# Attention with local windows and compressed entries, and a product in fp8: narrower turns of P, entries alternating with feed-forward products, batch 0's products moved into batch 3

## The chip, the cores and the metric

The kernel runs on one core of one Trainium2 chip. The metric is its time on the device in microseconds (us): the median over runs.

## The reference

For each of 4 batches of 1024 rows and 512 columns, x is normalised by row to xn, and the output is x + attention(xn) + product(xn).

```python
q  = rope(rmsnorm(xn @ Wq + bq))                 # 16 heads of 128
e  = softmax-weighted sums of 4 rows of xn       # 256 "entries"
ck, cv = rope(rmsnorm(e @ Wk + bk)), e @ Wv + bv
sparse = softmax of the 8 largest causal q.ck, times cv
lk, lv = rope(rmsnorm(xn @ Wlk + blk)), xn @ Wlv + blv
local  = softmax over own and previous block of 128 keys, times lv
attention = (sparse + local) / 2 @ Wo + bo
product   = fp8(xn * s) / s @ (fp8(input2 * s1) / s1)
```

## The kernel before, in words

The work is cut into 256 *units*, numbered u: batch u // 64, pair of heads (u // 8) % 8, block of 128 rows u % 8. A software pipeline runs over steps s. In step s TensorE projects q and lk of unit s (`proj_qk`, 24 matmuls of 512 columns in two halves: L520 to L522, four of each to a unit), turns and projects for unit s - 1 (`tr`, `proj_v`), and does the scores of s - 2, the turn of the probabilities P of s - 3 (`turn_p`, L576), the values of s - 4 (L591 with cv, the compressed values, and L594 with v) and the output product of s - 5 (`out_proj`, L606 to L608). f32 factors are kept as two rounded halves, hi and lo, multiplied in three matmuls; P, the entries and the values are plain f32, where one matmul is issued as two records with a load (LDWEIGHTS) each; turns are one.

Beside the units there are *tiles*: 32 blocks of 128 rows of x, eight to a batch. Batch 0's are prepared in steps -9 to 2. Tile t of a later batch is prepared one batch ahead, every seventh step from `tile_base(t)` on, by the delays in `LAGS` and, for four tiles together, `BLOCK_LAGS`: statistics (`norm_stats`, DVE), the power -0.5 of the variance (`power_x`, POOL), normalising, turning x, entries (`et`: four f32 matmuls with xt as the stationary and 32 columns of wm as the moving operand, L636), then ck and cv of a block (`ckv`, `turn_ck`). The feed-forward product of a tile is four bf16 matmuls of 512 columns (`ffn`, L662) on a quantised tile; `ffn_base(t)` sets its step, with `excess` and `rejoin` (DVE) and `quant_nan` (POOL) ahead of it and `init` (DVE) behind, which adds it to x. For tiles 0 to 7 it is done in batch 0 (steps 13, 20, ... 62) and added into `acc`, the sum of the batch in SBUF; for later tiles into `ini`, which is parked in HBM and loaded into `acc` at the batch's start. Input 2 is quantised in steps 4 to 9 in the same way.

During batch 0 the weights are split into halves (POOL `split` for Wq, Wlk, Wlv; ACT `hi_wo` and DVE `lo_wo` for Wo, in step 8g + 4 of group g) through the two buffers `wr`, and copied to HBM (`keep`, `keep_wo`), from where batches 1 to 3 fetch them.

Each engine executes its own list in order, written out as a loop over s; semaphores join them. Positions matter here. DVE's step: masks and maxima of s - 2 (`mask_max`, `max8`, `neg_max`), `lo_x` and `init`, `lo_c` of s - 4, `put_qk` (adds the bias to the projection), `lo_qk`, the sums for the norms, `add_out` of s - 5, and last the tile's statistics, `normalise`, `lo_wo`, `excess`, `rejoin`. POOL's: `rope_b`, `rope_rest`, `quant_nan`, `power_x`, `power_qk` (which ScalarE's `kscale` needs), `keep_8` and `normalise_p` of s - 2, which fills P's unused columns with zeros first, then `split`. ACT's: `put_et`, `hi_c`, the exponentials, copies, `kscale`, `hi_wo`, `cast_w2`. PSUM has a bank T for turns (`tr`, `turn_x`) and a bank Y for the output product, entries, ckv and feed-forward; `free` holds what TensorE has to wait for before it writes a bank. SP issues all of the large DMAs, in the order of its own loop.

Of the kernel before, what the change touches and what calls it, by code (L numbers as in the profile page):

```python
# [70 lines left out]

def unit_at(s, lag):
    return s - lag if 0 <= s - lag < NU else None


def tile_base(t):
# [5 lines left out]
        "max": (2, 2, 3), "ew": (3, 3, 4), "wm": (3, 3, 4), "et": (3, 4, 6), "park": (3, 3, 4)}  # L82
# [4 lines left out]
def tile_at(s, stage):  # L87
    for t in range(NTT):
        if tile_base(t) + LAGS[stage][min(t // 4, 2)] == s:
            return t  # L90
    return None


def block_at(s, stage):
    for k in range(NTT // 4):
        if tile_base(4 * k + 3) + BLOCK_LAGS[stage][min(k, 2)] == s:
            return k
    return None


def ffn_base(t):

    return 10 + 7 * t if t < 8 else tile_base(t) + 5
# [46 lines left out]
def build(nc, x, Wq, bq, Wcmp, bcmp, Wk, bk, Wv, bv, Wlk, blk, Wlv, blv, qnw, knw, Wo, bo,  # L150
# [9 lines left out]
    with ctx:  # L160
# [58 lines left out]
        kepto = nc.dram_tensor("kepto", (NG, 2, 2, 128, 512), F32, kind="Internal").ap()  # L219
        inis = nc.dram_tensor("inis", (NTT, 128, 512), F32, kind="Internal").ap()  # L220
# [98 lines left out]
        def run_sync(e):  # L319
# [100 lines left out]
            def store(u):  # L420
                b, i = u // 64, u % 8
                if b == 0:
                    e.wait_ge(S["bo0"], i + 1)
                else:
                    e.wait_ge(S["acc"], u + 1)
                e.dma_start(out[b, i * 128:(i + 1) * 128, :], acc[:, i, :]).then_inc(S["d_o%d" % i], 16)
# [32 lines left out]
            for s in range(FIRST, LAST):  # L459
# [34 lines left out]
            for i in range(NT):  # L494
                e.wait_ge(S["d_o%d" % i], 16 * NB)

        def run_tensor(e):
# [70 lines left out]
            def turn_p(u, h):  # L570
                a = 2 * u + h
                e.wait_ge(S["norm"], a + 1)
                if a >= 2:
                    e.wait_ge(S["p"], a - 1)
                for n, k in enumerate(pblocks(u)):
                    last = e.transpose(bP[h][:, n * 128:(n + 1) * 128], P[:, u % 2, h, k * 128:(k + 1) * 128], ident)  # L576
                last.then_inc(S["pt"], 1)

            def values(u, h):
                b, i = u // 64, u % 8  # L580
                ts_ = units_of(u)
                if h == 0:
# [48 lines left out]
            def entries(t):  # L631
                e.wait_ge(S["wm"], t + 1)
                if free["Y"]:
                    e.wait_ge(S[free["Y"][0]], free["Y"][1])
                for kt in range(KT):
                    last = e.matmul(bY[:, kt * 32:(kt + 1) * 32], xt[:, t % XR, kt * 128:(kt + 1) * 128], wm[:, :],  # L636
                                    start=True, stop=True)
                last.then_inc(S["et"], 1)
                free["Y"] = ("put_et", t + 1)
# [36 lines left out]
            for s in range(LAST):  # L676
# [12 lines left out]
                if tile_at(s, "et") is not None:  # L689
                    entries(tile_at(s, "et"))  # L690
                if ffn_at(s, 3) is not None:
# [21 lines left out]
        def run_scalar(e):  # L713
# [115 lines left out]
            def put_et(t):  # L829
# [3 lines left out]
                e.activation(et[:, :, (t % 4) * 32:(t % 4 + 1) * 32], bY[:, 0:128].rearrange("p (k c) -> p k c", k=KT),  # L833
# [45 lines left out]
            for s in range(LAST):  # L879
# [38 lines left out]
                if 4 <= s < 4 + KT:  # L918
                    cast_w2(s - 4)
# [3 lines left out]
        def run_vector(e):  # L923
# [105 lines left out]
            def add_out(u):  # L1029
# [8 lines left out]
                if u < 64 and u + 5 >= ffn_base(u % 8) + 3:  # L1038
                    e.wait_ge(S["init"], ffn_pos(u % 8) + 1)
# [77 lines left out]
            def init(t, s):  # L1117
                a = rows(t)
                e.wait_ge(S["ff"], ffn_pos(t) + 1)
                e.wait_ge(S["xn"], t + 1)  # L1120
                if t < 8:
                    done = [u for u in range(t, 64, 8) if u < s - 5]
                    if done:
                        e.wait_ge(S["acc"], done[-1] + 1)
# [55 lines left out]
            for s in range(LAST):  # L1180
# [3 lines left out]
                if u2 is not None:  # L1184
# [5 lines left out]
                    neg_max(u2)  # L1190
                if tile_at(s, "lo") is not None:
                    lo_x(tile_at(s, "lo"))
                if ffn_at(s, 3) is not None:
                    init(ffn_at(s, 3), s)
# [41 lines left out]
                if 5 <= s < 5 + KT:  # L1236
                    excess(s - 5)
                    rejoin(s - 5)
# [6 lines left out]
        def run_gpsimd(e):  # L1245
# [31 lines left out]
            def normalise_p(u, h):  # L1277
                C, top_ = width(u), 128 * (u % 8 // 4 + 1)
# [88 lines left out]
            for s in range(FIRST, LAST):  # L1367
# [10 lines left out]
                if 6 <= s < 6 + KT:  # L1378
                    quant_nan(s - 6)
# [97 lines left out]
```

## Time and profile before

| | |
|---|---|
| median of 3 runs | 2566.69 us (2566.32 to 2568.03) |
| the profiled execution | 2566.6 us, span 2564.8 us |
| granted TensorE clock, mean | 0.997 |
| PE busy | 2515.7 us (98%) |
| PEld, DVE | 2216.1 us, 1984.2 us (77%) |
| ACT, POOL | 1652.2 us (64%), 1565.7 us (61%) |
| DMA | 220.74 MB, 25.6% of 16 engines' time |

The span is the time from the first to the last instruction on the core. PE is TensorE's matmuls and PEld its weight loads, which overlap them; DVE is VectorE, ACT ScalarE, POOL GpSimd, SP SyncE. L576 is line 576 of the kernel. Batch 0 begins at 39.55 us (unit 0), batch 1 at 686.6, batch 2 at 1310.1, batch 3 at 1933.6.

### The profile page before, as it was taken

How to read it: one execution, taken by the hardware profiler on the slowest of the kernel's cores; microseconds unless marked ns; L12 is line 12 of the kernel's file. 1: busy time of each engine (PE TensorE's matmuls, PEld its weight loads, DVE VectorE, ACT ScalarE, POOL GpSimd, SP SyncE). 2: the span in 40 equal slices, each digit the busy share in tenths (PEclk: the TensorE clock that was granted, in tenths of full speed). 3: DMA queues.
4: the chain of work that ended last, by engine and by line, in shares of the span. 5: the costliest groups of instructions: out<-in, count | busy, mean ns of one | idle time of the engine just before them, and what ended most of it. 6: DMA issues, size and time to landing. Idle time of an engine off the chain costs nothing. (4 is left out here: it accounts for less than half of the span.)

```text
span 2564.8 us, 54971 instructions
## 1 busy us (share of the span) xinstructions
PE 2515.7 (98%) x15288; PEld 2216.1 (86%) x15320; DVE 1984.2 (77%) x6309; ACT 1652.2 (64%) x4674; POOL 1565.7 (61%) x2766
## 2 busy tenths in 40 slices
PE   6999999999999999999999999999999999999998
PEld 5888888888888888888888888888888888888887
DVE  6888888888878778777877778777877776676775
ACT  4666666566666666666666666666666666666665
POOL 5777777776676555555556655555556655555554
PEclk9999999999999999999999999999999999999999
DMA  3532233224332212022243122122143221122101
GB/s 109 169 104 71 96 104 115 89 70 135 116 125 87 86 56 91 30 99 79 86 147 115 43 87 87 59 87 65 65 132 122 81 71 63 38 71 71 61 11 50
DMA packets 168291, 220.74 MB, mean 86 GB/s; under 512 B 17842, under 2 KB 89012, under 8 KB 167988
## 3 DMA queue, kind: packets, MB, share of 16 engines
q1 hardware_dynamic: 167412, 216.96, 25.6%
q8 instruction: 126, 2.06, 0.3%
q14 instruction: 177, 1.45, 0.2%
q10 hardware_dynamic: 576, 0.26, 0.0%
HBM read 156.35 MB, written 60.82 MB: 85 GB/s over the span
## 5 line engine op out<-in xcount | busy, mean ns | idle before, releaser
L1298 POOL TENSOR_TENSOR t<-raw,tB 128x128 f32<-128x128 f32 x512 | 227.4, 465 | 592.2 <-DVE raw L930 591.8
L1252 POOL TENSOR_TENSOR r<-ss,mh 128x4 f32<-128x4 f32 x256 | 286.6, 1120 | 260.4 <-DVE ss L947 260.3
L779 ACT ACTIVATE ch<-bVC,blT 128x128 fp32r<-128x128 f32 x512 | 159.7, 363 | 435.8 <-PE bVC L594 435.0
L520 PE MATMUL bQK<-wh,xh 128*128 128x512 f32 x1024 | 426.7, 417 | 0.8 <-DVE raw L930 0.8
L521 PE MATMUL bQK<-wl,xh 128*128 128x512 f32 x1024 | 404.1, 395 | 0.0
L522 PE MATMUL bQK<-wh,xl 128*128 128x512 f32 x1024 | 401.9, 393 | 0.0
L975 DVE CUSTOM_DVE_ANT_0 P<-bS,cst 128x256 f32<-128x256 f32 (+1 forms) x512 | 203.7, 398 | 157.3 <-PE bS L568 156.8
L536 PE MATMUL bVC<-wh,xh 128*128 128x256 f32 x1024 | 311.1, 304 | 5.7 <-DVE cl L1024 5.7
L746 ACT ACTIVATE P<-P,nm,r 128x256 f32<-128x256 f32 (+1 forms) x512 | 295.3, 583 | 0.0
L740 ACT ACTIVATE raw<-raw,r 128x128 f32<-128x128 f32 x512 | 177.9, 395 | 177.0 <-POOL r L1252 172.4
L538 PE MATMUL bVC<-wh,xl 128*128 128x256 f32 x1024 | 289.8, 283 | 0.0
L537 PE MATMUL bVC<-wl,xh 128*128 128x256 f32 x1024 | 289.7, 283 | 0.0
L1024 DVE SCALAR_TENSOR_TENSOR cl<-bVC,blT,ch 128x128 fp32r<-128x128 f32 x512 | 155.7, 346 | 169.3 <-ACT ch L779 168.7
L1287 POOL TENSOR_SCALAR P<-P,rs 128x256 f32<-128x256 f32 (+1 forms) x512 | 257.7, 503 | 20.1 <-POOL P L1274 10.9
L957 DVE TENSOR_TENSOR qkl<-bT,qkh 128x512 fp32r<-128x512 f32 x256 | 177.1, 692 | 115.8 <-ACT qkh L718 115.3
L594 PEld LDWEIGHTS bVC<-pt,v 128*128 128x128 f32 x1920 | 254.5, 191 | 13.4
L594 PE MATMUL bVC<-pt,v 128*128 128x128 f32 x1920 | 255.5, 275 | 0.0
L726 ACT ACTIVATE pt<-bP 128x512 f32<-128x512 f32 (+2 forms) x512 | 239.9, 523 | 2.5 <-PE bP L576 2.4
L576 PEld LDWEIGHTS bP<-cst,P 128*128 128x128 f32 x1728 | 204.6, 141 | 35.9 <-POOL P L1288 0.9
L522 PEld LDWEIGHTS bQK<-wh,xl 128*128 128x128 f32 x1024 | 192.8, 188 | 44.7
L576 PE MATMUL bP<-cst,P 128*128 128x128 f32 x1728 | 231.2, 273 | 0.2 <-POOL P L1288 0.2
L606 PE MATMUL bY<-woh,ch 128*128 128x512 f32 x512 | 224.1, 438 | 6.3 <-DVE ini L1125 4.8
(144 smaller groups left out, 6941.2 us busy)
## 6 DMA issues: line engine op xcount, KB each, us to landing
wh<-kept SPq DMA_DIRECT2D x144, 256.0 KB, 4.1
wl<-kept SPq DMA_DIRECT2D x144, 256.0 KB, 4.5
kept<-wh SPq DMA_DIRECT2D x48, 256.0 KB, 3.1
kept<-wl SPq DMA_DIRECT2D x48, 256.0 KB, 3.3
woh<-kepto SPq DMA_DIRECT2D x48, 256.0 KB, 3.3
wol<-kepto SPq DMA_DIRECT2D x48, 256.0 KB, 3.8
out<-acc SPq DMA_DIRECT2D x32, 256.0 KB, 2.2
ini<-in_hidden_states SPq DMA_DIRECT2D x24, 256.0 KB, 4.6
```

Source lines behind the costliest of these rows:

```text
L520: e.matmul(bQK[:, :], a, b, start=kt == 0, stop=False)
L521: e.matmul(bQK[:, :], a, bl, start=False, stop=False)
L522: last = e.matmul(bQK[:, :], al, b, start=False, stop=kt == 3)
L536: e.matmul(bVC[:, 0:256], a, b, start=kt == 0, stop=False)
L537: e.matmul(bVC[:, 0:256], a, bl, start=False, stop=False)
L538: last = e.matmul(bVC[:, 0:256], al, b, start=False, stop=kt == KT - 1)
L576: last = e.transpose(bP[h][:, n * 128:(n + 1) * 128], P[:, u % 2, h, k * 128:(k + 1) * 128], ident)
L594: last = e.matmul(dst, v_[:, t % 4, h, :], pt[:, h, n * 128:(n + 1) * 128], start=False, stop=n == len(ts_) - 1 and h == 1)
L726: e.activation(pt[:, h, 0:n], bP[h][:, 0:n], ACT.Copy).then_inc(S["p"], 1)
L746: e.activation(pl, pl, ACT.Exp, scale=r4[:, u % 4, 2 * h:2 * h + 1], bias=nm[:, u % 4, h, 1:2], accum_out=su[:, u % 4, h, 1:2]).then_inc(S ...
L1252: e.tensor_tensor(r4[:, u % 4], ss[:, u % 4], mh[:, 0:4], ALU.pow).then_inc(S["r4"], 1)
L1287: e.tensor_scalar(pl, pl, rs[:, u % 4, h, 1:2], 0.5, ALU.mult, ALU.mult)
```

## The change

- `turn_p` turns only `last_rows(u)` columns of P's last block (68, 68, 96, 128 for u % 4 = 0 to 3; 128 in units 0, 1 and 4), `values` multiplies with as many rows of cv and pt, and `normalise_p` fills only up to there.
- Entries of tiles from 8 on go to bank T and two steps later (lag 8 for 6), but for the last tile of a batch. Where they meet a feed-forward product in one step, `entries_ffn` issues both in turn, an f32 entry matmul and then a 512-column bf16 one. Even blocks from the second batch on are two steps later.
- The feed-forward products of tiles 0 to 7 are at steps 201, 208, ... 250. Batch 0's sum goes to `part` in HBM and comes back into `ini` for `init`; SP stores the result.
- `lo_wo` is in the next step behind `neg_max`; `keep_wo` is a step later. `power_x` is behind `normalise_p` in steps from 0 on.
- Input 2 is loaded and quantised two steps earlier.

```diff
+def last_rows(u):
+    return 128 if u in (0, 1, 4) else max(68, width(u) - 128 * (u % 8 // 4))

-        "max": (2, 2, 3), "ew": (3, 3, 4), "wm": (3, 3, 4), "et": (3, 4, 6), "park": (3, 3, 4)}
+        "max": (2, 2, 3), "ew": (3, 3, 4), "wm": (3, 3, 4), "et": (3, 4, 8), "park": (3, 3, 4)}
 def tile_at(s, stage):
+        early = 2 if stage == "et" and t >= 8 and t % 8 == 7 else 0
+        if tile_base(t) + LAGS[stage][min(t // 4, 2)] - early == s:
 def block_at(s, stage):
+        late = 2 if k >= 2 and k % 2 == 0 else 0
+        if tile_base(4 * k + 3) + BLOCK_LAGS[stage][min(k, 2)] + late == s:
 def ffn_base(t):
-    return 10 + 7 * t if t < 8 else tile_base(t) + 5
+    return 64 * (NB - 1) + 6 + 7 * t if t < 8 else tile_base(t) + 5

 # SP
+                    e.dma_start(part[i], acc[:, i, :]).then_inc(S["d_o%d" % i], 16)   # batch 0
+            def fetch_part(t):
+                e.wait_ge(S["d_o%d" % t], 16)
+                if t < 2:
+                    e.wait_ge(S["d_is"], 16 * (NTT - 8))
+                else:
+                    e.wait_ge(S["d_f"], 16 * (t - 1))
+                e.dma_start(ini[:, t % 2, :], part[t]).then_inc(S["d_i%d" % (t % 2)], 16)
+            def store_whole(t):
+                e.wait_ge(S["init"], ffn_pos(t) + 1)
+                e.dma_start(out[0, t * 128:(t + 1) * 128, :], ini[:, t % 2, :]).then_inc(S["d_f"], 16)
-                    if kind == "o" and split_at + 1 == s:
+                    if kind == "o" and split_at + 2 == s:
                         keep_wo(gi, c)
-                if 2 <= s < 2 + KT:
-                    load_w2(s - 2)
+                if 0 <= s < KT:
+                    load_w2(s)
+                if t is not None and t < 8:            # t = ffn_at(s, 5)
+                    store_whole(t)
+                if ffn_at(s, 1) is not None and ffn_at(s, 1) < 8:
+                    fetch_part(ffn_at(s, 1))

 # TensorE
+                    r = last_rows(u) if k == pblocks(u)[-1] else 128
+                    last = e.transpose(bP[h][0:r, n * 128:(n + 1) * 128], P[:, u % 2, h, k * 128:k * 128 + r], ident)
+                        r = last_rows(u) if n == i // 4 else 128
+                        e.matmul(bVC[:, 256:512], cv[0:r, b % 2, n, :], pt[0:r, :, c], start=n == 0, stop=False)
+            def entries_ffn(t, f):
+                e.wait_ge(S["wm"], t + 1)
+                e.wait_ge(S[free["T"][0]], free["T"][1])
+                e.wait_ge(S["q8"], 4 + ffn_pos(f) + 1)
+                e.wait_ge(S[free["Y"][0]], free["Y"][1])
+                for kt in range(KT):
+                    c = slice(kt * 128, (kt + 1) * 128)
+                    m = e.matmul(entries_of(t)[:, kt * 32:(kt + 1) * 32], xt[:, t % XR, c], wm[:, :], start=True, stop=True)
+                    if kt == KT - 1:
+                        m.then_inc(S["et"], 1)
+                    last = e.matmul(bY[:, :], q8[:, ffn_pos(f) % QR, c], w2q[:, kt, :], start=kt == 0, stop=kt == KT - 1)
+                last.then_inc(S["ff"], 1)

 # ScalarE, VectorE, GpSimd
-                if 4 <= s < 4 + KT:
-                    cast_w2(s - 4)
+                if 2 <= s < 2 + KT:
+                    cast_w2(s - 2)
                     neg_max(u2)
+                for q, c in enumerate(CHUNKS):
+                    if c[0] == "o" and c[3] == s - 1:
+                        lo_wo(q)
                 if tile_at(s, "lo") is not None:
-                for q, c in enumerate(CHUNKS):         # at the end of the step
-                    if c[0] == "o" and c[3] == s:
-                        lo_wo(q)
-                C, top_ = width(u), 128 * (u % 8 // 4 + 1)
+                C, top_ = width(u), 128 * (u % 8 // 4) + last_rows(u)
-                if tile_at(s, "power") is not None:
+                if s < 0 and tile_at(s, "power") is not None:
                     power_x(tile_at(s, "power"))
                     normalise_p(u2, 1)
+                if s >= 0 and tile_at(s, "power") is not None:
+                    power_x(tile_at(s, "power"))
```

`excess`, `rejoin` and `quant_nan` of input 2 move by two steps with `cast_w2`; `init` takes `ini` for all tiles.

## Rows read from the trace of the kernel before

**Rows 1.** Busy us and instructions by stretch: PE, PEld, DVE, ACT, POOL; PEclk, DMA, GB/s.
```profile
39.55:686.60 647.05, 624.10 (x3738) 542.20 (x3753) 532.27 (x1614) 413.41 (x1168) 465.92 (x746) 0.99 0.31 104
1933.60:2545.00 611.40, 611.33 (x3746) 543.38 (x3746) 435.25 (x1461) 391.91 (x1111) 338.45 (x650) 1.00 0.19 64
```

**Rows 2.** The same view, of L520 on TensorE alone, in six stretches.
```profile
39.55:114.89 75.34, 14.04 (x32) 0.94 0.43 141
114.89:199.73 84.84, 13.78 (x32) 0.97 0.28 92
199.73:686.60 486.87, 79.77 (x192) 1.00 0.30 100
765.74:842.06 76.32, 13.29 (x32) 1.00 0.22 73
842.06:1310.09 468.03, 79.79 (x192) 1.00 0.25 82
2012.74:2087.44 74.70, 13.29 (x32) 1.00 0.18 61
```

**Rows 3.** Weight loads by line: busy us, mean ns of one | idle before.
```profile
L576 PEld LDWEIGHTS bP<-cst,P 128*128 128x128 f32 x1728 | 204.6, 141 | 35.9 <-POOL P L1288 0.9 <-issue 0.2
...
L591 PEld LDWEIGHTS bVC<-pt,cv 128*128 128x128 f32 x768 | 138.8, 189 | 21.0 <-ACT pt L726 3.6 <-issue 2.3
...
L662 PEld LDWEIGHTS bY<-w2q,q 128*128 128x128 bf16 x128 | 10.0, 98 | 12.7 <-issue 4.2
```

**Rows 4.** TensorE in time, a unit of batch 3: start, us, line, op.
```profile
2114.50 1.03 PE L576 MATMUL bP<-cst,P 128*128 128x128 f32 x8
...
2115.49 0.28 PE L537 MATMUL bVC<-wl,xh 128*128 128x256 f32 x1
2115.61 0.28 PE L538 MATMUL bVC<-wh,xl 128*128 128x256 f32 x1
```

**Rows 5.** TensorE in time, around the entries of a tile.
```profile
834.32 0.97 PE L636 MATMUL bY<-wm,xt 128*128 128x32 f32 x8
835.12 0.68 PE L591 MATMUL bVC<-pt,cv 128*128 128x256 f32 x2
835.64 0.61 PE L594 MATMUL bVC<-pt,v 128*128 128x128 f32 x4
```

**Rows 6.** TensorE in time, around a feed-forward product.
```profile
923.02 0.81 PE L662 MATMUL bY<-w2q,q 128*128 128x512 bf16 x3
923.67 1.03 PE L591 MATMUL bVC<-pt,cv 128*128 128x256 f32 x4
924.53 0.72 PE L594 MATMUL bVC<-pt,v 128*128 128x128 f32 x5
```

**Rows 7.** Waits of TensorE: total us, times, longest.
```profile
PE bY L606 <- DVE ini L1125: 4.8, 4, 3.1
```

**Rows 8.** Engines in time, units 44 and 45; idle before in brackets.
```profile
493.37 0.56 POOL L1256 TENSOR_TENSOR st<-st,mh 128x1 f32<-128x1 f32 x1 [2.71 <-DVE st L1055]
494.94 0.70 ACT L740 ACTIVATE raw<-raw,r 128x128 f32<-128x128 f32 x2 [4.14 <-POOL r L1252]
496.19 1.40 DVE L1045 TENSOR_TENSOR wol<-wr,woh 128x512 fp32r<-128x512 f32 x2 [2.90 <-ACT woh L789]
499.93 0.47 PE L606 MATMUL bY<-woh,ch 128*128 128x512 f32 x1 [3.08 <-DVE ini L1125]
```

**Rows 9.** Engines in time, units 60 and 61, then 9, then 8.
```profile
656.82 1.40 DVE L1045 TENSOR_TENSOR wol<-wr,woh 128x512 fp32r<-128x512 f32 x2 [1.26 <-ACT woh L789]
661.34 0.63 PE L546 MATMUL bT<-cst,raw 128*128 128x128 f32 x4 [2.20 <-DVE xsl L1074]
...
136.16 0.51 PE L536 MATMUL bVC<-wh,xh 128*128 128x256 f32 x1 [1.81 <-DVE cl L1024]
...
120.54 0.72 ACT L811 ACTIVATE a<-ini,isc 128x512 fp8e4<-128x512 f32 x1 [1.85 <-DVE qb L1098]
```

**Rows 10.** DMA issues: KB of one, median us to landing.
```profile
wr<-in_Wlv SPq DMA_DIRECT2D x16, 256.0 KB, 3.9
```

More of the change, by code:

```diff
@@ L219, in build @@
         kepto = nc.dram_tensor("kepto", (NG, 2, 2, 128, 512), F32, kind="Internal").ap()
+        part = nc.dram_tensor("part", (NT, 128, 512), F32, kind="Internal").ap()
         inis = nc.dram_tensor("inis", (NTT, 128, 512), F32, kind="Internal").ap()
@@ L282, in logits_of, with entries_of @@
             return (bY if t >= FIRST_TILES else bS[1])[:, 0:128]
+        def entries_of(t):
+            return (bY if t < 8 else bT)[:, 0:128]
         def bias_of(u, h):
@@ L423, in store @@
                     e.wait_ge(S["bo0"], i + 1)
-                else:
-                    e.wait_ge(S["acc"], u + 1)
-                e.dma_start(out[b, i * 128:(i + 1) * 128, :], acc[:, i, :]).then_inc(S["d_o%d" % i], 16)
+                    e.dma_start(part[i], acc[:, i, :]).then_inc(S["d_o%d" % i], 16)
+                    return
+                e.wait_ge(S["acc"], u + 1)
+                e.dma_start(out[b, i * 128:(i + 1) * 128, :], acc[:, i, :]).then_inc(S["d_o%d" % i], 16)
+            def fetch_part(t):
+                e.wait_ge(S["d_o%d" % t], 16)
+                if t < 2:
+                    e.wait_ge(S["d_is"], 16 * (NTT - 8))
+                else:
+                    e.wait_ge(S["d_f"], 16 * (t - 1))
[3 more added lines that the diff above has]
+                e.dma_start(out[0, t * 128:(t + 1) * 128, :], ini[:, t % 2, :]).then_inc(S["d_f"], 16)
             load_acc(0)
@@ L632, in entries @@
                 e.wait_ge(S["wm"], t + 1)
-                if free["Y"]:
-                    e.wait_ge(S[free["Y"][0]], free["Y"][1])
+                bank = "Y" if t < 8 else "T"
+                if free[bank]:
+                    e.wait_ge(S[free[bank][0]], free[bank][1])
                 for kt in range(KT):
-                    last = e.matmul(bY[:, kt * 32:(kt + 1) * 32], xt[:, t % XR, kt * 128:(kt + 1) * 128], wm[:, :],
+                    last = e.matmul(entries_of(t)[:, kt * 32:(kt + 1) * 32], xt[:, t % XR, kt * 128:(kt + 1) * 128], wm[:, :],
                                     start=True, stop=True)
                 last.then_inc(S["et"], 1)
-                free["Y"] = ("put_et", t + 1)
+                free[bank] = ("put_et", t + 1)
+            def entries_ffn(t, f):
[10 more added lines that the diff above has]
+                last.then_inc(S["ff"], 1)
+                free["T"] = ("put_et", t + 1)
+                free["Y"] = ("init", ffn_pos(f) + 1)
             def ckv(k):
@@ L688, in run_tensor @@
                     ckv(block_at(s, "kv"))
-                if tile_at(s, "et") is not None:
+                if tile_at(s, "et") is not None and ffn_at(s, 3) is not None:
+                    entries_ffn(tile_at(s, "et"), ffn_at(s, 3))
+                elif tile_at(s, "et") is not None:
                     entries(tile_at(s, "et"))
-                if ffn_at(s, 3) is not None:
+                elif ffn_at(s, 3) is not None:
                     ffn(ffn_at(s, 3))
@@ L1037, in add_out @@
                     e.wait_ge(S["bo"], u // 64 * 8 + u % 8 - 7)
-                if u < 64 and u + 5 >= ffn_base(u % 8) + 3:
-                    e.wait_ge(S["init"], ffn_pos(u % 8) + 1)
                 e.tensor_tensor(a, bY[:, :], a, ALU.add).then_inc(S["acc"], 1)
@@ L1115, in weights4, with init @@
                                 ALU.mult).then_inc(S["wm"], 1)
-            def init(t, s):
-                a = rows(t)
+            def init(t):
+                a = ini[:, t % 2, :]
                 e.wait_ge(S["ff"], ffn_pos(t) + 1)
-                e.wait_ge(S["xn"], t + 1)
                 if t < 8:
-                    done = [u for u in range(t, 64, 8) if u < s - 5]
-                    if done:
-                        e.wait_ge(S["acc"], done[-1] + 1)
+                    e.wait_ge(S["d_i%d" % (t % 2)], 16 * (t // 2 + NTT // 2 - 1))
+                else:
+                    e.wait_ge(S["xn"], t + 1)
                 e.scalar_tensor_tensor(out=a, in0=bY[:, :], scalar=isc[:, 4:5], in1=a, op0=ALU.mult,
@@ L1193, in run_vector @@
                 if ffn_at(s, 3) is not None:
-                    init(ffn_at(s, 3), s)
+                    init(ffn_at(s, 3))
                 if u4 is not None:
@@ L1235, in run_vector @@
                     rejoin(KT + ffn_pos(ffn_at(s, 1)))
-                if 5 <= s < 5 + KT:
-                    excess(s - 5)
-                    rejoin(s - 5)
+                if 3 <= s < 3 + KT:
+                    excess(s - 3)
+                    rejoin(s - 3)
                 if s == 0:
```

11 lines of the change are left out of this document (4 added, 7 removed), and 2 rows, old and new, of the table SIGNALS.

## The prediction

> **What bounds the kernel.** I read the engines' busy times by stretch first [rows 1]. TensorE is busy 611.33 of 611.40 us in batch 3 and 624.10 of 647.05 us in batch 0; VectorE, the next, has 435 and 532 us. So only TensorE's own work and its stalls cost time, and the stalls lie in batch 0. Second I count work periods by the projection's matmuls, four L520 to a unit [rows 2]: eight units take 74.70 us where nothing is added (batch 3), and units 16 to 63 of batch 0 take 486.87 us where units 80 to 127 of batch 1, with the same tiles in the same places, take 468.03. Third come loads and matmuls of single groups [rows 3 to 6], for what each edit is worth on a full TensorE, and last the waits and two places in batch 0 where a wait travels through the engines to TensorE [rows 7 to 9].
>
> **Narrower turns.** For 189 units (three quarters of 256, less three exempt ones) the last block of P is turned with 68 or 96 columns as the stationary operand instead of 128, in both heads: 378 turns, 19,096 columns fewer. The moving operand stays the identity's 128 columns. The eight turns of a unit start at 2114.50; L537 is at 2115.49, and a 256-column matmul ahead of it takes 0.12 (2115.49 to 2115.61), so the eight took 0.87, 0.109 each [rows 4]. Is that the load or the stream? The entries' matmuls move only 32 columns, so there the load sets the pace: eight of them from 834.32, and L591 with two matmuls of 0.215 ends at 835.64, so 835.21 - 834.32 = 0.89, 0.111 each (0.215 is 0.86/4, the four L591 of the next group) [rows 5, 6]. A turn's load is listed with 141 ns where an ordinary f32 load has 189 [rows 3]: 0.048 shorter. So a turn's load takes about 0.111 - 0.048 = 0.063 of the 0.109, and the rest of the pace is the stream of 128 identity columns, which stays. Bounds: if the 0.109 were all load and in proportion to the columns, 19,096 x 0.109/128 = 16.3 us would go; on the other side nothing excludes a loss, priced below. I take 0, since the load's own row is nearest. The values' matmul with fewer rows of cv keeps its 128 stationary and 256 moving columns: 0. The fill of P on GpSimd gets shorter; it is off the path, hidden by TensorE.
>
> The Trainium skill, "TensorE: Matmul & The Clock Gate", section "LDWEIGHTS", says the opposite of my choice: a load takes the stationary's column count over 1.2 GHz. By that sentence a 68-column load takes 57 ns instead of 107, and the turns would give some 16 us. Its 107 ns agrees with the entries' 0.111, but the listed turn load is shorter than that rule allows for 128 columns, and no row here has fewer.
>
> **Entries alternating with feed-forward products.** Tiles 8 to 31 now have their entries in the step of their feed-forward matmuls, but for the last tile of each batch (its entries stay two steps earlier): 7 x 3 = 21 pairs. Apart they cost 0.89 (above) and 4 x 0.216 = 0.87 (L662: 923.67 - 923.02 = 0.65 for three) [rows 6]: 1.76. Interleaved, the first entry load of each round is hidden behind the 512-column product before it. On the path are the second entry load, 0.111, the bf16 load and the product, 0.216. The bf16 load is listed with 98 ns against 189 [rows 3], 0.091 less, so about 0.02 of its own. A round is 0.35, four are 1.39 to 1.42. Gain 0.34 x 21 = 7.1. Bounds: with the bf16 load at its full 0.098, 4 x 0.425 = 1.70 and 1.3 us in all; with it free, 4 x 0.327 and 9.5 us. f32 and bf16 already follow each other in [rows 6] without a gap, so I see no loss. I take 7. New waits: bank T needs lo_qk of the step before, which is done before the scores; ScalarE's put_et now waits about 0.5 longer, ahead of hi_c, but hi_c waits for the values' matmuls behind the pair anyway.
>
> **Feed-forward of batch 0 moved to batch 3.** Eight products of 0.87, 6.9 us of TensorE, leave a batch and enter another: 0. Its VectorE work (excess, rejoin, init) and GpSimd work go where those engines have room: VectorE is busy 435 of 611 us there [rows 1]. Added DMAs: acc to part instead of out (the same), eight fetches and eight stores of 256 KB. On SP's queue fetch_part waits only for old transfers, and store_whole waits for an init two steps earlier; behind it stand weight fetches which have half a unit group of slack. 0.
>
> **Power and low halves in batch 0.** Units 16 to 63 are 486.87 - 468.03 = 18.84 us longer than their twins; seven products explain 7 x 0.87 = 6.1, so 12.7 is stall [rows 2]. The chain of its largest piece [rows 8]: GpSimd stands at power_x (L1256) for 2.71 us until VectorE's statistics at its step's end, so power_qk is late, ScalarE's kscale starts after 4.14 idle, hi_wo follows it, VectorE waits 2.90 for woh at the end of its step, begins the next step late, init is late, and TensorE's L606 stands 3.08. The change takes power_x behind keep_8 and normalise_p and the low halves into the next step behind neg_max, where VectorE otherwise idles ahead of lo_c. Both links are cut, and that init is gone too. The second piece, L546 2.20 behind xsl, has 1.26 of waiting for woh and 1.40 of lo_wo ahead of it in VectorE's order, and rejoin besides [rows 9]. What is late next: lo_wo's 1.4 now stands ahead of lo_x and lo_c in eight steps (I leave 0.5 there for some), and the weight buffer is released some 5 us later, so the next chunk lands at about +5 + 3.9 [rows 10] of a 10 us step, just when GpSimd wants to split it; chunk loads, keeps and load_ini queued behind it on SP shift with it. I take back 9 of 12.7, bounds 4 and 12.7. In batches 1 and 2 the same wait for ini costs L606 three times 1.7 in all beside the 3.1 [rows 7]; power_x's move takes 1.2 of it, bounds 0 and 1.7.
>
> **Input 2 quantised two steps earlier.** Units 8 to 15 take 84.84 against 76.32, of which one product 0.87: 7.7 us of stall, in part by a lower granted clock (0.97 of 2.4 GHz on average in the row), and units 0 to 7 take 75.34, more than eight full units, though the first four have no values and no output product [rows 2]. The rows show how: cast_w2 waits 1.85 for VectorE's qb, so hi_c, lo_c and L536 are late (1.81) [rows 9]. The same work now falls in units 2 to 7. There TensorE's units are shorter, so VectorE and ScalarE bind, but tile 8's statistics no longer meet it. It doesn't vanish; I take 6, bounds -2 and 12.
>
> **Sum.** 7 + 9 + 1.2 + 6 = 23.2 us off the profiled execution's 2566.6 (span 2564.8 and 1.8 around it), which lies 0.1 under the median of the runs: 2543.4. The forecast's own range adds the bounds in part: 2536 to 2551.
>
> **Rivals.** (1) Narrow loads shorten the turns, -16.3 more: 2527. For it: 0.109 and 0.111 are nearly one pace; against: the turn's load is listed 48 ns shorter. (2) Batch 0 gives little back: stalls of lo_wo ahead of lo_c, of the late chunk and of the quantisation in units 2 to 7 take the place of the old. Then 4 - 2 + 7 = 9 of gain: 2558. For it: VectorE is at 532 of 647 us in batch 0 [rows 1] and none of the work goes away but eight products'; against: both cut links are seen in [rows 8]. (3) Slower: a stationary operand narrower than 128 makes TensorE empty itself before and after it. Place: each narrow turn (two sides, two heads) and the cv matmuls (two sides), 6 times in 189 units, 1134 times. Price: a turn takes 0.27 from start to end and its pace is 0.109 (1.03 - 7 x 0.109) [rows 4], so 0.16 each: +181, 2725 us. It makes the change slower from 23/1134 = 0.02 us each. For it and against it there is no row: all stationary operands here have 128 columns.
>
> The Trainium skill, "TensorEngine Tiling (Array Packing)", section "Key Properties", says that changing the tiling mode drains TensorE; its modes are 128, 64 and 32, and 68 and 96 fit in 128 only, so by it (3) doesn't happen. No run here shows a drain.
>
> **Chances.** Forecast 0.57, (1) 0.22, (2) 0.16, (3) 0.05. The 8-in-10 range reaches into (1) and (2): 2522 to 2559. A measurement here tells 0.2%, 5 us; the first three cases all lie beyond it, but for a tail of (2): faster 0.93, same 0.02, slower 0.05.
>
> **What would show it.** Turns: eight in a unit still 0.87 long (0.77 by (1)), and eight plain units still 74.7 in late batch 3 (74.2 by (1)). Pairs: 1.4 in a step that had 0.87, none for entries alone in batches 1 and 2 but at the last tile. Batch 0: no 3 us hole at unit 45; units 16 to 63 about 486.9 - 6.1 - 9 - 7 x 0.34 = 469 (seven of the pairs lie in them). Units 0 to 15 153 instead of 160. Batch 3 6.9 longer. I am wrong if eight plain units change by over 0.1 us, if a pair takes 1.7, or if units 16 to 63 stay above 476.

## The result, and the profile after

The changed kernel takes 2547.93 us (2547.14 to 2548.24), the kernel before in the same session 2566.66 (2566.32 to 2568.03): ratio 0.9921 [0.991, 0.9933], 18.7 us faster. The forecast was 23.2 us, to 2543.4, so the time is 4.5 us above it and inside the likeliest case's own range.

The profiled execution took 2547.14 us, with a span of 2545.3 (before: 2564.8). First, as before, busy time against the span, from the page of the changed kernel.

```profile
PE 2509.3 (99%) x15320; PEld 2220.3 (87%) x15320; DVE 1975.3 (78%) x6309; ACT 1658.7 (65%) x4674; POOL 1540.3 (61%) x2702
```

TensorE's busy time fell by 6.4 (2515.7 before), the span by 19.5: two thirds of what went was standing. Where, the stretches tell. The next rows answer to [rows 2]: windows of the projection's first matmul, four to a unit (L520, now L550), with length, busy time, granted clock, DMA share and GB/s. They are units 0 to 7, 8 to 15, 16 to 63, 128 to 191, 200 to 207 and 208 to 215.

```profile
38.16:118.98 80.82, 15.10 (x32) 6.96 (x33) 0.87 0.36 123
118.98:195.19 76.21, 13.30 (x32) 6.07 (x33) 1.00 0.33 107
195.19:663.55 468.36, 79.90 (x192) 36.43 (x193) 1.00 0.31 104
1284.59:1905.13 620.54, 106.51 (x256) 48.55 (x257) 1.00 0.26 86
1984.29:2059.93 75.64, 13.33 (x32) 6.07 (x33) 1.00 0.20 67
2059.93:2136.42 76.49, 13.31 (x32) 6.07 (x33) 1.00 0.20 66
```

The same cuts in both traces add up to the whole difference (batches 1 and 2 were 623.5 each before; units 192 to 254 were 592.6, are 599.9; the tail is unit 255 and what follows):

| stretch | before | after | difference | forecast |
|---|---|---|---|---|
| until unit 0 | 39.55 | 38.16 | -1.4 | 0 |
| units 0 to 15 | 160.19 | 157.03 | -3.2 | -6.9 |
| units 16 to 63 | 486.87 | 468.36 | -18.5 | -17.5 |
| batches 1 and 2 | 1247.0 | 1241.6 | -5.4 | -6.0 |
| batch 3 to unit 254 | 592.6 | 599.9 | +7.3 | +6.9 |
| tail | 38.55 | 40.27 | +1.7 | 0 |

Two readings stand in it. Units 16 to 63 now take about what units 80 to 127 took in [rows 2] (468.03); those have got shorter too, to 465.93, so 2.4 of the 12.7 us of stall are left. Units 0 to 15 gave back half of what was forecast: units 8 to 15 fell from 84.84 to 76.21, units 0 to 7 rose from 75.34 to 80.82, at a mean clock of 0.87 for 0.94. Of this rise 2.9 lies in units 0 and 1 (19.01 before, 21.88 after). Unit 1 ran mostly at half clock in this profile (mean 0.58) and took 9.23 for 6.55; in kernels with the same code there it takes 6.6 to 9.7 (below), so this part is not the change's doing as far as these runs show. Units 2 to 15 by themselves fell from 141.17 to 135.15.

One shift of work is in the table, too: tile 8's entries (0.89) stood in unit 15 and now stand in unit 17, so units 0 to 15 lost them and units 16 to 63 got them.

The 3 us wait of L606 at unit 45 [rows 7, 8] is gone. Between unit 2 and unit 254 the longest waits of TensorE are now these, from the view of waits (L576 is the turn of ck and the q side of `tr`, L638 the first output matmul, L566 the projection of values). The first two are in unit 5, the third in unit 4; from unit 6 on none is over 0.4:

```profile
PE bT L576 <- DVE qkl L1201: 2.4, 1, 2.4
PE bY L638 <- DVE wol L1094: 2.1, 1, 2.1
...
PE bVC L566 <- DVE cl L1075: 0.6, 1, 0.6
```

The pair that `entries_ffn` makes, in time on TensorE (answers to [rows 5, 6]):

```profile
831.39 0.30 PE L682 MATMUL bT<-wm,xt 128*128 128x32 f32 x2
831.53 0.38 PE L685 MATMUL bY<-w2q,q 128*128 128x512 bf16 x1
831.75 0.30 PE L682 MATMUL bT<-wm,xt 128*128 128x32 f32 x2
...
832.60 0.38 PE L685 MATMUL bY<-w2q,q 128*128 128x512 bf16 x1
832.82 1.03 PE L623 MATMUL bVC<-pt,cv 128*128 128x256 f32 x4
```

From 831.39 to L623 at 832.82 it is 1.43 for what took 1.76 apart; a round is 0.36 (831.39 to 831.75). The turns (L576 is now L607) and the cv matmuls' loads, by form, with busy time and mean ns of one (answers to [rows 3]; L685 is the pair's bf16 load):

```profile
L607 PEld LDWEIGHTS bP<-cst,P 128*128 128x128 f32 x1350 | 168.2, 140 | 32.7 <-POOL P L1336 0.9 <-issue 0.2
...
L623 PEld LDWEIGHTS bVC<-pt,cv 68*128 68x128 f32 x250 | 46.5, 190 | 3.7
...
L607 PEld LDWEIGHTS bP<-cst,P 128*68 128x68 f32 x250 | 28.2, 113 | 2.8
...
L607 PEld LDWEIGHTS bP<-cst,P 128*96 128x96 f32 x128 | 16.3, 127 | 0.0
...
L685 PEld LDWEIGHTS bY<-w2q,q 128*128 128x128 bf16 x84 | 15.2, 181 | 0.0
```

The loads did get shorter: 140, 127 and 113 ns for 128, 96 and 68 columns, 0.45 ns a column. The next section asks whether anything follows from that.

### The profile page after: what moved, and what is told of

The parts are those of the page before. It is cut to its first block, busy times and chain, and to the rows that moved or that the text cites. A ratio compares the mean times of both kernels' runs of the same rounds, so it can differ in the third digit from the quotient of the medians.

```text
span 2545.3 us, 54963 instructions
## 1 busy us (share of the span) xinstructions
PE 2509.3 (99%) x15320; PEld 2220.3 (87%) x15320; DVE 1975.3 (78%) x6309; ACT 1658.7 (65%) x4674; POOL 1540.3 (61%) x2702
## 4 chain that ended last, share of the span: by engine, by line
PE 74%; DMA 0%; POOL 0%; issue 0%; SPq 0%; ACT 0%; DVE 0%; ACTq 0%; POOLq 0%; DVEq 0%
PE bQK L550 7%; PE bQK L551 7%; PE bQK L552 7%; PE bVC L626 6%; PE bP L607 6%; PE bVC L623 5%; PE bY L638 4%; PE bVC L566 4%; PE bVC L568 4%; PE bVC L567 4%; PE bY L639 4%; PE bY L640 4%; PE bT L576 3%; PE bS L598 3%; PE bS L597 3%; PE bS L596 3%
## 5 line engine op out<-in xcount | busy, mean ns | idle before, releaser
L550 PE MATMUL bQK<-wh,xh 128*128 128x512 f32 x1024 | 427.8, 418 | 0.8 <-DVE raw L981 0.8
L566 PE MATMUL bVC<-wh,xh 128*128 128x256 f32 x1024 | 310.6, 303 | 0.6 <-DVE cl L1075 0.6
L567 PE MATMUL bVC<-wl,xh 128*128 128x256 f32 x1024 | 289.5, 283 | 0.0
L1335 POOL TENSOR_SCALAR P<-P,rs 128x256 f32<-128x256 f32 (+1 forms) x512 | 246.7, 482 | 35.5 <-POOL P L1322 22.2
L607 PE MATMUL bP<-cst,P 128*128 128x128 f32 (+2 forms) x1728 | 231.1, 273 | 0.4 <-POOL P L1336 0.4
L607 PEld LDWEIGHTS bP<-cst,P 128*128 128x128 f32 (+2 forms) x1728 | 200.3, 135 | 35.5 <-POOL P L1336 0.9
L638 PE MATMUL bY<-woh,ch 128*128 128x512 f32 x512 | 224.9, 439 | 3.7 <-DVE wol L1094 2.1
```

The source lines that it names most:

```text
L550: e.matmul(bQK[:, :], a, b, start=kt == 0, stop=False)
L566: e.matmul(bVC[:, 0:256], a, b, start=kt == 0, stop=False)
L567: e.matmul(bVC[:, 0:256], a, bl, start=False, stop=False)
L607: last = e.transpose(bP[h][0:r, n * 128:(n + 1) * 128], P[:, u % 2, h, k * 128:k * 128 + r], ident)
L638: e.matmul(bY[:, :], a, woh[:, h, :], start=h == 0, stop=False)
L1335: e.tensor_scalar(pl, pl, rs[:, u % 4, h, 1:2], 0.5, ALU.mult, ALU.mult)
```

## The experiments

Each kernel is the changed one with one edit, unless said otherwise. The medians scatter (the kernel before had 2566.66 to 2569.89 beside the different runs), and with them the stretches at a lower clock near the two ends, so differences of a few us are read from stretches of units, each from one profiled execution. Where a unit's length is given without a row, it is the distance from its first projection matmul to the next unit's.

**Turns: full width.**

```diff
-    return 128 if u in (0, 1, 4) else max(68, width(u) - 128 * (u % 8 // 4))
+    return 128
```

> The changed kernel (2547.9 us) with P's last block turned and multiplied with all 128 columns and rows again, and filled with zeros to there. Theory: a turn's pace of 0.109 us is the stream of the identity's 128 columns, its load (listed 48 ns shorter than an ordinary f32 load) hides behind it. Then nothing changes: 2547.9 within 1 us, and eight turns of a unit take 0.87 us in both. Rival 1, the load sets the pace: 16 us slower, 2564. Third: the shorter zero fill on GpSimd is what counts, in batch 0 alone: 1 to 3 us slower, all of it in units 0 to 63.

2544.26 us, ratio 0.9907 [0.9893, 0.992]; its interval overlaps the changed kernel's. Windows of units 16 to 63 and 128 to 191:

```profile
194.47:662.39 467.92, 79.79 (x192) 36.42 (x193) 1.00 0.32 104
1282.67:1902.93 620.26, 106.38 (x256) 48.58 (x257) 1.00 0.26 86
```

They are 0.4 and 0.3 shorter than with narrow turns (468.36, 620.54), and units 200 to 207 take 75.59 for 75.64. So the narrow turns give nothing and cost about 0.05 in eight units, 1.5 us over 240 units; all of units 16 to 254 together differ by 1.8. The other 2.4 us of the span's difference (4.2) lie ahead of unit 16 and in the tail, where kernels with the same code there differ as much (below). Rival 1 falls, and the choice of 0 stands.

**Turns: a shorter stream.** If the moving operand paces a turn, shortening that one must show. On the kernel with full turns, from unit 8 on; it leaves out the last 60 queries of the block:

```diff
-    last = e.transpose(bP[h][0:r, n * 128:(n + 1) * 128], P[:, u % 2, h, k * 128:k * 128 + r], ident)
+    m = 68 if u >= 8 and k == pblocks(u)[-1] else 128
+    last = e.matmul(bP[h][0:r, n * 128:n * 128 + m], P[0:m, u % 2, h, k * 128:k * 128 + r], ident[0:m, 0:m],
+                    start=True, stop=True, is_transpose=True)
```

> The changed kernel with full turns (the run at 2544.3 us), and from unit 8 on the last block's turn moves 68 identity columns instead of 128, while its stationary keeps all 128 columns of P (68 of its 128 rows). It leaves out the last 60 queries of that block. 496 turns are touched. Theory: the stream of the moving columns is a turn's pace, so each takes (128 - 68) x 0.107/128 = 0.050 less until the load (0.063) binds, 0.045 to 0.050: 22 to 25 us faster, 2519 to 2522, and eight plain units of batch 3 go from 74.7 to 73.95. Rival 1, the load of 128 stationary columns sets the pace: no change, 2544.

2533.87 us, ratio 0.9869 [0.9854, 0.9884], 10.4 below full turns. Six turns of one unit, first in the kernel with full turns, then with the short ones, and the matmul behind them:

```profile
2121.69 0.82 PE L607 MATMUL bP<-cst,P 128*128 128x128 f32 x6
2122.26 0.36 PE L566 MATMUL bVC<-wh,xh 128*128 128x256 f32 x1
```

```profile
2112.64 0.72 PE L608 MATMUL bP<-cst,P 128*128 128x128 f32 x6
2113.17 0.36 PE L566 MATMUL bVC<-wh,xh 128*128 128x256 f32 x1
```

One turn of the two sides' last ones saves 0.044 (0.57 to 0.53), the other does not: from the second side's last turn to the second matmul behind it (L567) it is 0.23 in both. An ordinary load stands there, and I take its 0.111 [rows 5] for what paces. 248 units times 0.044 are 10.9. I had expected both to save. Units 128 to 191 are 2.75 shorter than with full turns, 0.043 a unit:

```profile
1277.33:1894.84 617.51, 106.37 (x256) 48.58 (x257) 1.00 0.26 86
```

What follows is that the 128 identity columns of the stream, not the load of P, hold a turn at 0.109; the load is hidden under them, and so was every column that the change took from it. The short turn's stationary also lost 60 of its 128 rows; its load is listed as before (140 ns for 141), and no run takes the two apart:

```profile
L608 PEld LDWEIGHTS bP<-cst,P 68*128 68x128 f32 x496 | 69.6, 140 | 2.8
```

**Turns: 64 columns.** Does a narrower stationary make TensorE empty itself (rival 3)?

```diff
-    return 128 if u in (0, 1, 4) else max(68, width(u) - 128 * (u % 8 // 4))
+    return 128 if u in (0, 1, 4) else max(64, width(u) - 128 * (u % 8 // 4))
```

> The changed kernel with 64 columns and rows in place of 68 where the last block has 32 or 64 entries. Theory: the load isn't the pace, and 64 is like 68: 2547.9 within 1 us. Rival 3, that a narrower stationary makes TensorE empty itself before and after: at 64, where 68 still counted as full width, it would show now, in 125 units, 6 times each, 0.16 us each: 120 us slower, 2668. A half of that, if only the turns or only the loads count, still is 2600 or more.

2594.15 us, ratio 1.0101 [1.0087, 1.0115]: 46 us slower than with 68. The loads by form, and loads in time around one unit's cv matmuls:

```profile
L607 PEld LDWEIGHTS bP<-cst,P 128*64 128x64 f32 x250 | 27.8, 111 | 2.8
...
L623 PEld LDWEIGHTS bVC<-pt,cv 64*128 64x128 f32 x250 | 36.8, 184 | 36.0 <-issue 36.0
```

```profile
2176.20 0.41 PEld L623 LDWEIGHTS bVC<-pt,cv 128*128 128x128 f32 x2
2176.94 0.29 PEld L623 LDWEIGHTS bVC<-pt,cv 64*128 64x128 f32 x2 [0.33 <-issue]
2177.57 0.97 PEld L626 LDWEIGHTS bVC<-pt,v 128*128 128x128 f32 x8 [0.33 <-issue]
```

The turns with 64 columns are not the cause: their loads idle 2.8 us in all, as those of 68 columns do. It is the values' matmul, whose stationary then has 64 rows. Its load stands 0.33 with nothing to wait for, and so does the first full load behind it; for 68 and 96 rows there is no such gap. Units 216, 217, 220 and 221, which have 64 rows, are 0.37 to 0.41 longer than with 68, the others not at all. So what rival 3 feared exists, on the rows, at 64, at some 0.2 for each of two changes a unit (an estimate: half of 0.37 to 0.41), and the 68 in the code keeps clear of it.

The Trainium skill, "TensorEngine Tiling (Array Packing)", section "Key Properties", says that a change of tiling mode drains TensorE. The 64-row load with its 0.33 us on each side agrees, and the 68- and 96-row loads agree with my reading that they stay in mode 128; the 64-column turn, which runs at full pace, does not show such a drain.

**Pairs undone.** Entries back in their own step.

```diff
-        "max": (2, 2, 3), "ew": (3, 3, 4), "wm": (3, 3, 4), "et": (3, 4, 8), "park": (3, 3, 4)}
+        "max": (2, 2, 3), "ew": (3, 3, 4), "wm": (3, 3, 4), "et": (3, 4, 6), "park": (3, 3, 4)}
...
-        early = 2 if stage == "et" and t >= 8 and t % 8 == 7 else 0
+        early = 0
...
-        late = 2 if k >= 2 and k % 2 == 0 else 0
+        late = 0
```

> The changed kernel with the entries of tiles 8 to 31 two steps earlier again (and the even blocks with them), so that no entries meet a feed-forward product; bank T and all else stay. Theory: each of 21 pairs costs 1.43 us against 0.89 + 0.87 apart, 0.33 saved: 2547.9 + 7.0 = 2555. Rival, the pair's gain is spacing of VectorE's work (the ck chain two steps later) and not the loads: then less than 3 us in all, and batches 1 and 2 not 2.3 us longer each.

2554.41 us, ratio 0.9948 [0.9935, 0.996], 6.5 slower. Units 128 to 191, with seven pairs undone:

```profile
1287.87:1910.76 622.89, 106.50 (x256) 48.56 (x257) 1.00 0.26 86
```

2.35 more than the changed kernel's 620.54: 0.34 each, the step's own size. In units 16 to 63 it is 1.7 (470.05), because tile 8's entries (0.89) are back in unit 15, which takes 10.36 for 9.47; with them it is 2.6 for seven.

**Feed-forward products back in batch 0.**

```diff
-    return 64 * (NB - 1) + 6 + 7 * t if t < 8 else tile_base(t) + 5
+    return 10 + 7 * t if t < 8 else tile_base(t) + 5
```

with `init` on `acc` and without `fetch_part` and `store_whole`.

> The changed kernel with the feed-forward products of tiles 0 to 7 back in batch 0 (steps 13 to 62), added into acc, and batch 0 stored directly. Theory (the prediction's step): 6.9 us of TensorE work only change place, and the stalls of batch 0 are gone by the other edits: 2547.9 within 2 us. Rival: the product's VectorE and GpSimd work in batch 0 is what made the stalls of units 33 to 61, beside the power and the low halves: 4 to 8 us slower, all in units 16 to 63.

2548.3 us, ratio 0.9925 [0.9912, 0.9939]: the same. Units 16 to 63 (the line is L545 there):

```profile
197.14:673.52 476.38, 75.46 (x192) 36.40 (x192) 1.00 0.31 103
```

8.0 more than after, for seven products of 0.87 (6.1): leaving batch 0 took 1.9 of stall with it. Units 192 to 254 are 7.0 shorter in return (592.96 for 599.92). Moving work between stretches that TensorE fills is worth nothing, as costed.

**Low halves of Wo, and the power.** First `lo_wo` back at the end of its step and `keep_wo` a step earlier; then `power_x` back ahead of `power_qk`; then both.

```diff
-                for q, c in enumerate(CHUNKS):
-                    if c[0] == "o" and c[3] == s - 1:
-                        lo_wo(q)
...
+                for q, c in enumerate(CHUNKS):
+                    if c[0] == "o" and c[3] == s:
+                        lo_wo(q)
```

> The changed kernel with the low halves of Wo at the end of VectorE's step again, and keep_wo a step earlier; power_x stays behind normalise_p. Theory: power_x was the first link of the chain of unit 45, so woh now comes in time and lo_wo's place is worth only its 1.3 us where VectorE is the late engine: 1 to 3 us slower in units 16 to 63, some of it taken back in unit 5, 2547 to 2550. Rival: lo_wo's place carries most of the 10 us that units 16 to 63 gained beside products and pairs: 2553 or more.

```diff
-                if s < 0 and tile_at(s, "power") is not None:
+                if tile_at(s, "power") is not None:
                     power_x(tile_at(s, "power"))
...
-                if s >= 0 and tile_at(s, "power") is not None:
-                    power_x(tile_at(s, "power"))
```

> The changed kernel with power_x ahead of power_qk again; the low halves stay in the next step. Theory: GpSimd again stands for the tile's statistics, r, kscale and hi_wo are late, but lo_wo in the next step behind neg_max has room for it: 3 to 6 us slower in batch 0, and 0.6 in each of batches 1 and 2 at the out-projection behind init: 2552 to 2555. Rival: with lo_wo moved the link is cut anyway, and power_x's place is worth under 1.5 us: 2549 or less.

> The changed kernel with both power_x and the low halves in their old places. Theory: the two are links of one chain, so that both together cost more than their sum: units 16 to 63 get back most of the 10 us of stall, less what the products' leaving took (2 us by the run with the products in batch 0): 2555 to 2558. Rival: their costs are separate and simply add: the sum of the two runs before.

The medians are 2548.13 (ratio 0.9921 [0.9908, 0.9935]), 2548.8 (0.9924 [0.9911, 0.9936]) and 2554.91 (0.9943 [0.993, 0.9955]). The first two are not told apart from the changed kernel, and the third's interval just touches its [0.991, 0.9933], so the stretches decide. Units 16 to 63 of the three, one after the other:

```profile
199.74:667.43 467.69, 79.97 (x192) 36.42 (x193) 1.00 0.31 104
```

```profile
196.60:666.54 469.94, 79.96 (x192) 36.44 (x193) 1.00 0.31 103
```

```profile
198.92:671.31 472.39, 79.95 (x192) 36.43 (x193) 1.00 0.31 103
```

Against 468.36 the old `lo_wo` alone gives 0.7 back, the old power costs 1.6, both together 4.0. The wait at unit 45 says why; it is none in the changed kernel and in the first of these, and in the second and the third:

```profile
487.96 0.47 PE L638 MATMUL bY<-woh,ch 128*128 128x512 f32 x1 [0.74 <-DVE ini L1173]
```

```profile
492.29 0.47 PE L638 MATMUL bY<-woh,ch 128*128 128x512 f32 x1 [2.31 <-DVE ini L1173]
```

Behind the wait of 2.31 TensorE runs at half clock for 3.4 (493.60 to 497.01), which is part of the third's 4.0. The two are links of one chain [rows 8]: together they cost more than the sum of the single ones (4.0 against 0.9). Cutting the power's link alone removes all of it, cutting the low halves' alone 2.4 of the 4.0. The power's move is the one that counts in units 16 to 63. The move of the low halves pays elsewhere: without it units 0 to 7 take 84.59 instead of 80.82. The first row below is that window in the kernel with the old `lo_wo`. Its unit 5 has one wait of 5.00 where the changed kernel has two of 2.40 and 2.13 (second row) and is hardly longer (16.93 for 16.58). The difference falls in unit 7, 12.93 for 9.47: VectorE is still behind with the quantisation there, L566 waits for its `lo_c` (third row), and TensorE goes to half clock (120.51 to 123.92).

```profile
38.65:123.24 84.59, 15.10 (x32) 7.05 (x33) 0.86 0.36 123
```

```profile
94.79 1.09 PE L576 MATMUL bT<-cst,raw 128*128 128x128 f32 x4 [5.00 <-DVE qkl L1201]
...
120.52 0.58 PE L566 MATMUL bVC<-wh,xh 128*128 128x256 f32 x1 [1.81 <-DVE cl L1075]
```

**Input 2 at its old place.**

```diff
-                if 2 <= s < 2 + KT:
-                    cast_w2(s - 2)
+                if 4 <= s < 4 + KT:
+                    cast_w2(s - 4)
```

and the loads, `excess`, `rejoin` and `quant_nan` two steps later as well.

> The changed kernel with input 2 loaded and quantised in its old steps (loads 2 to 5, casts 4 to 7, VectorE's part 5 to 8). In the changed kernel units 8 to 15 are 7.7 us shorter by stalls, but units 4 and 5 are 7.6 us longer (8.85 and 16.58 against 7.35 and 10.53). Theory: the early quantisation put ScalarE's casts of step 4 behind hi_wo and ahead of hi_ck, for which VectorE's lo_ck waits at the start of its step 5, and lo_wo is in that step too; taken back, units 4 and 5 fall to about 7.4 and 11, and units 7 to 12 grow by 6 to 8 us: 2548 to 2551 in all. Rival: the hole in unit 5 is lo_wo's alone (moved into step 5); then it stays, the stalls of units 7 to 12 come back too, and the time is 2554 or more.

2548.38 us, ratio 0.9919 [0.9905, 0.9932]: no difference. Units 0 to 7 and 8 to 15:

```profile
40.46:117.50 77.04, 15.63 (x32) 7.20 (x33) 0.91 0.40 133
117.51:197.62 80.11, 13.30 (x32) 6.07 (x33) 1.00 0.31 101
```

Together 157.15 against the changed kernel's 157.03. So the step for which I took 6 us is worth 0.1 (0.4 without units 0 and 1). It did take 3.9 out of units 8 to 15 and 1.8 out of unit 7, and it put 5.2 into units 4 and 5 (20.25 here, 25.43 in the changed kernel). What shortened units 2 to 15 by 6.0 was mainly the rest: the product (0.87) and tile 8's entries (0.89) that left, and the new place of the low halves (units 2 to 15 take 139.21 without it, 135.15 with it, 4.1 for it). What the early place meets, the changed kernel's unit 5 shows. VectorE and ScalarE in time there (idle before in brackets):

```profile
88.50 1.13 ACT L840 ACTIVATE woh<-wr 128x512 fp32r<-128x512 f32 x2
89.54 0.70 ACT L862 ACTIVATE a<-ini,isc 128x512 fp8e4<-128x512 f32 x1
90.15 0.70 ACT L863 ACTIVATE b<-ini,isc 128x512 fp8e4<-128x512 f32 x1
90.76 0.36 ACT L910 ACTIVATE qkh<-bT 128x256 fp32r<-128x256 f32 x1
```

```profile
91.15 0.42 DVE L1201 TENSOR_TENSOR qkl<-bT,qkh 128x256 fp32r<-128x256 f32 x1 [1.40 <-ACT qkh L910]
...
93.05 1.28 DVE L1094 TENSOR_TENSOR wol<-wr,woh 128x512 fp32r<-128x512 f32 x2
94.25 0.60 DVE L1075 SCALAR_TENSOR_TENSOR cl<-bVC,blT,ch 128x128 fp32r<-128x128 f32 x2
```

```profile
91.72 0.63 PE L576 MATMUL bT<-cst,raw 128*128 128x128 f32 x4 [2.40 <-DVE qkl L1201]
94.48 0.76 PE L638 MATMUL bY<-woh,ch 128*128 128x512 f32 x1 [2.13 <-DVE wol L1094]
```

Step 4 has a half of Wo and a quarter of input 2 on ScalarE in one row, then the high half of ck. ck's low half and with it TensorE's turn stand 2.40; behind that `lo_wo` holds the first output product for 2.13. With input 2 at its old place the first wait is 1.12 and the second 2.13 as well, and unit 5 has no half clock and takes 12.89 for 16.58: the 2.13 is the low halves' price and not input 2's.

```profile
90.71 0.63 PE L576 MATMUL bT<-cst,raw 128*128 128x128 f32 x4 [1.12 <-DVE qkl L1201]
93.47 0.47 PE L638 MATMUL bY<-woh,ch 128*128 128x512 f32 x1 [2.13 <-DVE wol L1094]
```

And in the changed kernel TensorE, having stood, gets half its clock a little later:

```profile
92.70:99.50 6.80, 5.02 (x17) 4.34 (x18) 6.73 (x22) 4.63 (x12) 3.79 (x6) 0.50 0.66 222
```

In this stretch (busy PE, PEld, DVE, ACT, POOL; clock 0.50 of 2.4 GHz) VectorE is busy 6.73 of 6.80.

**Input 2 clear of step 4, three orders.** All on the kernel with full turns, with the four casts at steps 2, 3, 5, 7, then 2, 3, 6, 7, then 1, 2, 6, 7.

```diff
-                if 2 <= s < 2 + KT:
-                    cast_w2(s - 2)
+                if s in (2, 3, 5, 7):
+                    cast_w2((2, 3, 5, 7).index(s))
```

> The changed kernel with full turns (2544.3 us) and input 2 cast in steps 2, 3, 5, 7 instead of 2 to 5, the rest of its quantisation one and two steps later each. Theory: the hole of unit 5 (VectorE's lo_ck behind ScalarE's hi_ck behind the cast and hi_wo of step 4, then lo_wo) needs the cast of step 4 and VectorE's part of step 4 just ahead; without them unit 4 falls from 8.86 to 7.4 and unit 5 from 16.9 to 10, with no lower clock behind it: 7 to 9 us faster, 2535 to 2538. Rival: VectorE's work in units 2 to 8 is too much in any order, and the time moves into units 6 to 9: 2541 or more.

> The same with casts in steps 2, 3, 6, 7. Theory: unit 5 is emptier still than with a cast in step 5 (9.8), but two quantisations follow each other in units 7 and 8, where the kernel before had its holes of 1.8 us: 0 to 3 us slower than with 2, 3, 5, 7. Rival: only the ck chain of units 4 and 5 matters, then both are within 1 us.

> The changed kernel with full turns (2544.3 us) and the casts of input 2 in steps 1, 2, 6, 7, so that VectorE's part (excess, rejoin) is in steps 2, 3, 7, 8 and none in step 4 or 5. With 2, 3, 5, 7 unit 4 stayed at 8.84 and unit 5 at 14.33, although step 4 had no cast: VectorE's excess and rejoin of step 4 (88 to 90.6 us) still made its step 5 late, and lo_wo of 1.3 us came on top. Theory: VectorE's own load in step 4 is the cause; without it unit 4 falls to 7.4 and unit 5 to 12 or less: 3 to 6 us faster, 2538 to 2541, less 1 us for a hole in unit 10. Rival: lo_wo in step 5 behind a late hi_wo is enough for the hole: unit 5 stays above 14 and the time is 2544 or more.

2544.37 (0.9911 [0.9895, 0.9928]), 2542.88 (0.9905 [0.9891, 0.992]) and 2547.87 us (0.9924 [0.9911, 0.9938]), against 2544.26 with the casts at 2 to 5: none is told apart from it. I had expected unit 5 at 10 us in the first. It takes 14.33 there, 15.85 and 13.71 in the others, 16.93 with the casts at 2 to 5; units 0 to 7 take 79.0, 80.6 and 80.6 against 78.5. But in these three unit 1 fell into half clock (9.1 to 9.2 for 6.6) and units 0 and 1 are 2.7 to 3.2 longer; units 2 to 7 alone take 56.7, 58.2 and 58.7 against 59.4. So the first order does take 2.7 out of units 2 to 7 (3.6 out of units 2 to 15, 132.27 for 135.84), and its profile lost 3.2 ahead of them and 1.5 in the tail, both at half clock. Whether the order is worth anything in the median, these runs don't show. Unit 5 of the last, free of casts in steps 3 to 5:

```profile
92.42 0.63 PE L576 MATMUL bT<-cst,raw 128*128 128x128 f32 x4 [0.37 <-DVE qkl L1201]
95.18 0.47 PE L638 MATMUL bY<-woh,ch 128*128 128x512 f32 x1 [2.14 <-DVE wol L1094]
```

The 2.40 has become 0.37, but 2.14 for the low half of Wo stays, and its unit 4 takes 11.52 instead of 8.86. Most of the stall stays in any of these orders and changes its place. Fewer instructions in these units, or another engine for them, were not tried.

## Why the prediction was right, and which term was not

- **Turns, 0:** right, and the stream does keep the pace, as the shorter stream shows. Measured +1.5 to +1.8 us of cost. The Trainium skill, "TensorE: Matmul & The Clock Gate", section "LDWEIGHTS", has the load time go with the columns; the load rows agree in direction (140 to 113 ns for 128 to 68 columns), but at 0.45 ns a column where the rule has 0.83, and the pace did not follow.
- **Pairs, -7.1:** right in size, 1.43 a pair (1.39 to 1.42 said), 0.34 each in batch 2. Undoing them costs 6.5. Its small term was luck: I took 0.02 for the bf16 load because it was listed with 98 ns beside 189; in the pair it is listed with 181, and the round is 0.36 all the same. So the listed duration did not tell what this load costs on the path; the 0.063 that I worked out for a turn's load rests on the same reading and was not measured by itself.
- **Feed-forward moved, 0:** right in sum; 1.9 of stall that went with it from batch 0 belongs to the next step's 9.
- **Power and low halves, -9 in batch 0:** right in size, inside the bounds. Units 16 to 63 lost 18.5 and got tile 8's entries (0.9), which the forecast had overlooked; of the 19.4 that went, 6.1 are products, 2.4 pairs, 11.0 stall. Wrong in the picture of two equal cuts: undoing both costs 4.0, the power alone 1.6, the low halves -0.7. With the 1.9 of the feed-forward move, 5.9 of the 11.0 is assigned by undoing. Most of the rest is unit 61, the second piece of [rows 9]: 13.94 before, 10.58 after, and 10.88 with the products back, 9.90 with power and low halves both old. So that hole needed the products in batch 0 and the old places together, as far as these two kernels show, and either edit removes it. Some 2 us were not taken apart.
- **Power in batches 1 and 2, -1.2:** 5.4 less 14 pairs of 0.34 (4.8) leaves 0.6. The old place of the power costs 0.3 in units 128 to 191 (620.87 for 620.55). The 1.7 of waits that I had put into these batches holds one of 0.51 at unit 17, which is in batch 0; theirs are two of 0.62.
- **Input 2, -6: this is the step that failed.** It measured -0.1 in units 0 to 15. I took for cause of the stalls there that the quantisation met tile 8's statistics; the place it went to has shorter units, a half of Wo and ck's turn, which the prediction had named ("VectorE and ScalarE bind") and then priced at under 2 us of the 7.7. It cost 5.2 in units 4 and 5, about what the move gave in units 7 to 15. Rival 2 was right here, and wrong for units 16 to 63. That units 0 to 15 got shorter at all is due to the product, tile 8's entries and the low halves, whose 4.1 us in units 2 to 15 the prediction had not forecast: that the total came so near is in part luck.
- **Tail and start:** a stretch at half clock before the end (granted clock 0.50 in 2529.80 to 2533.20) costs 1.7. Kernels with the same code there have a tail of 38.6 or of 40.2, so it is not the change's doing as far as these runs show. The same holds for the time until unit 0, 38.2 to 40.5.

The table's forecasts add up to 23.5 us (the sum's 23.2 and rounding), the spans differ by 19.5. Of these 4.0 us 3.7 is units 0 to 15 (2.9 of it the longer units 0 and 1), 2.1 batch 3 with its tail (1.7 of it clock), 0.6 batches 1 and 2; 1.0 came back in units 16 to 63 and 1.4 before unit 0.

The fastest versions that compute everything are the changed kernel with full turns (2544.26) and the same with the casts at 2, 3, 6 and 7 (2542.88); the runs do not tell them apart.

## What to carry to other kernels

Before shortening an operand, find which of load and stream sets the pace: compare the distance of starts in two neighbours that differ in one of them, not the listed durations. A stall that travels through several engines can go when one link is cut (here the power's alone), so price the chain, not the links. And when work is moved out of a crowded step, add up what each engine has in the steps it goes to, in units of that place's own length; a move inside start-up only moved the hole.

## What the runs showed that I had not expected

- A stationary with 64 rows between full ones costs 0.37 to 0.41 us a unit, 46 us in all, where 68 rows cost nothing; 64 columns in a turn cost nothing either.
- A turn of 68 moving columns has a pace of 0.064 where 128 have 0.109, but only if the next one is a turn: with an ordinary f32 load behind it nothing is saved.
- Unit 1 took 9.2 us in the changed kernel and 6.6 with full turns, though unit 1's turns are full in both: it fell into half clock in one and not in the other. Units 0 and 1 of two profiles differ by up to 3.4 us, mostly for this, so stretches are better compared from unit 2 on.
